# A fused two-layer Flamingo block on one core: late side products copied out in their own step, expert matrices loaded as halves

## What is computed

```
x = x + tanh(g0) * xattn0(ctx, x)            # 8 heads, masked
x = x + tanh(g2) * moe(x)                    # w1, w3 [8,512,256], w2 [8,256,512]
      h1 = x w1^T ; h3 = x w3^T ; y = (silu(h1) * h3) w2^T, weighted by the router
x = x + tanh(g1) * xattn1(ctx, x)            # 16 heads
x = x + tanh(g3) * ffn(x)                    # act_quant / weight_quant, conv, gelu
```

## Time and profile before

| | us |
|---|---|
| median of 3 runs | 1510.13 (1507.44 to 1515.85) |
| the profiled execution | 1512.02 |
| its span, first to last instruction | 1510.3 |

### The profile page before, as it was taken

How to read it: one execution, slowest core, us unless ns; L and a number is a source line. 1 busy time by engine, 2 the same in 40 slices (tenths; PEclk the granted TensorE clock), 3 DMA queues, 4 the chain that set the end, 5 groups by cost and what they waited for, 6 DMA issues and landing times.

```text
span 1510.3 us, 45214 instructions
## 1 busy us (share of the span) xinstructions
PE 1266.9 (84%) x16920; PEld 984.6 (65%) x16920; DVE 1059.2 (70%) x2851; ACT 981.6 (65%) x2319; POOL 1087.2 (72%) x1346
## 2 busy tenths in 40 slices
PE   1888888678987878788999999899999999998863
PEld 1556665567766756556888787667666667666652
DVE  4777878856555567786666666777877778777645
ACT  2887877555555566545656565787777777777741
POOL 5887876767666654465777677788888888878763
PEclk9998989889999989989999999999999999999985
DMA  8689888589999958358999997454544544355320
GB/s 254 145 233 209 181 205 183 138 169 240 225 245 229 226 111 200 97 118 214 248 269 240 251 250 189 82 108 96 100 89 95 102 96 107 85 93 100 78 53 7
DMA packets 444426, 239.97 MB, mean 159 GB/s; under 512 B 389312, under 2 KB 423984, under 8 KB 436400
## 3 DMA queue, kind: packets, MB, share of 16 engines
q1 hardware_dynamic: 411720, 178.51, 57.5%
q10 hardware_dynamic: 29416, 51.22, 10.7%
q0 software_dynamic: 3072, 7.34, 1.8%
HBM read 107.78 MB, written 35.50 MB: 95 GB/s over the span
## 4 chain that ended last, share of the span: by engine, by line
PE 34%; ACT 17%; DVE 12%; issue 10%; DMA 9%; POOL 7%; SPq 5%; DVEq 3%; ACTq 2%; POOLq 0%; another core or an unknown queue 0%
PE bank_ring L1144 7%; DMA expert_up<-experts_up 6%; PE bank_ring L1182 5%; PE bank_ring L1130 5%; DVE scores L1411 5%; ACT scores L900 5%; PE bank_out L1163 4%; PE bank_x L1245 4%; ACT probs L907 3%; ACT values L927 3%; PE bank_scores L1104 2%; SPq L555 2%; POOL probs L692 2%; PE bank_x L1196 2%; ACT keys L920 2%
## 5 line engine op out<-in xcount | busy, mean ns | idle before, releaser
L692 POOL TENSOR_TENSOR probs<-scores,probs 112x487 f16<-112x487 f32 x373 | 414.1, 1127 | 221.7 <-ACT probs L907 217.0
L900 ACT ACTIVATE scores<-scores,score_min 112x487 f32<-112x487 f32 x384 | 266.3, 695 | 117.4 <-DVE score_min L1411 114.5
L1433 DVE SCALAR_TENSOR_TENSOR values<-bank_ring,values 128x512 f16<-128x512 f32 x192 | 132.4, 690 | 214.4 <-ACT values L927 214.0
L1411 DVE CUSTOM_DVE_ANT_0 scores<-bank_scores,mask 112x487 f32<-112x487 f32 x384 | 238.3, 658 | 2.5 <-PE bank_scores L1104 2.1
L907 ACT ACTIVATE probs<-scores 112x487 f16<-112x487 f32 x384 | 214.2, 606 | 17.1 <-DMA probs_turned<-probs 1.1
L927 ACT ACTIVATE values<-bank_ring 128x512 f16<-128x512 f32 x192 | 113.2, 590 | 134.6 <-PE bank_out L1163 132.5
L1144 PE MATMUL bank_ring<-weights,kv_B 128*128 128x128 f16 x3072 | 194.8, 220 | 2.1 <-DVE keys L1428 2.1
L1144 PEld LDWEIGHTS bank_ring<-weights,kv_B 128*128 128x128 f16 x3072 | 183.9, 99 | 11.3 <-DVE keys L1428 3.2
L1163 PE MATMUL bank_out<-values,probs_turned 128*128 128x64 f16 x4608 | 170.8, 195 | 17.1 <-issue 16.8
L1130 PE MATMUL bank_ring<-kv_B,weights 128*128 128x488 f16 x768 | 180.9, 372 | 0.0
L1163 PEld LDWEIGHTS bank_out<-values,probs_turned 128*128 128x128 f16 x4608 | 159.0, 99 | 20.7 <-issue 19.1
(11 more groups left out here) (236 smaller groups left out, 2424.9 us busy)
## 6 DMA issues: line engine op xcount, KB each, us to landing
expert_up<-experts_up SPq DMA_DIRECT2D x43, 1024.0 KB
expert_down<-experts_down SPq DMA_DIRECT2D x43, 512.0 KB, 6.7
raw_weights<-in_weights ACTq DMA_DIRECT2D x8, 1536.0 KB, 10.8
experts_up<-expert_up ACTq DMA_DIRECT2D x8, 1024.0 KB, 5.3
probs_turned<-probs SPq DMA_TRANSPOSE x384
context_turned_B<-kv_B ACTq DMA_DIRECT2D x16, 375.0 KB, 7.8
kv_B<-context_turned_B ACTq DMA_DIRECT2D x16, 375.0 KB, 4.0
moe_results<-moe_result SPq DMA_DIRECT2D x43, 128.0 KB, 4.4
```

Of the source, the lines that this page charges most:

```text
L692: pool.tensor_tensor(PR[:, u % 4, 1, 0:KEYS], S[:, u % 4, 0:KEYS], PR[:, u % 4, 0, 0:KEYS], ALU.subtract).then_inc(probs_split[u % 2], 1)
L900: act_e.activation(S[:, u % 4, 0:KEYS], S[:, u % 4, 0:KEYS], ACT.Exp, bias=rmin[:, u % 4:u % 4 + 1], scale=-1.0, accum_out=rsum[:, g % 2, ...
L1411: dve.tensor_tensor_reduce(out=S[:, u % 4, 0:KEYS], in0=bS[u % 2][0:TOK, 0:KEYS], in1=mask[:, m, 0:KEYS], scale=1.0, scalar=3.0e38, op0=AL ...
```

## The change

Two things, and what they need.

1. DVE reads the late products of step j in step j itself, behind the keys' split and ahead of `split_v(j)`, and no longer behind the masks of step j+1. The five small instructions behind the second `f_max` become a function `hidden_scale`; it stays in step j+1 (now behind `norm_out`), but for the last two sequences, where it stays with the read.
2. The up matrices of an expert are kept so that a first half (columns for the first 256 hidden units of w1 and w3) and a second half are each contiguous per partition, and are loaded with two DMAs of 512 KB and a semaphore each. The second half of tile i+1 is issued where the whole was. The first half of tile i+2 is issued in step i, between the two transposes of the probabilities. PE waits for each half on its own. The rounding and splitting of expert weights write two runs of 256 columns.

```diff
-                if part == 0:
+                if part < 2:
                     if t >= 2:
-                        sp.wait_ge(up_ready, 2 * (t - 2) + 2)
-                    sp.dma_start(eup[:, t % 2], up_dram[e]).then_inc(up_loaded[t % 2], 16)
+                        sp.wait_ge(up_ready, 2 * (t - 2) + part + 1)
+                    at = part * UP_WORDS // 2
+                    sp.dma_start(eup[:, t % 2, at:at + UP_WORDS // 2], up_dram[e][:, at:at + UP_WORDS // 2])\
+                        .then_inc(up_loaded[t % 2][part], 16)
...
                     if i == -2:
                         load_expert(b, 0, 0)
+                        load_expert(b, 0, 1)
                     if i == -1:
-                        load_expert(b, 0, 1)
+                        load_expert(b, 0, 2)
...
                     if 1 <= i + 1 < TILES[b]:
-                        load_expert(b, i + 1, 0)
+                        load_expert(b, i + 1, 1)
                     if 1 <= i < TILES[b]:
-                        load_expert(b, i, 1)
+                        load_expert(b, i, 2)
...
                 if is_pair(j):
-                    for u in (2 * j, 2 * j + 1):
-                        turn_probs(u)
+                    turn_probs(2 * j)
+                    for b in range(2):
+                        i = j - first_tile_step(b)
+                        if 1 <= i + 2 < TILES[b]:
+                            load_expert(b, i + 2, 0)
+                    turn_probs(2 * j + 1)
...
+                pe.wait_ge(up_loaded[t % 2][half], 16 * (t // 2 + 1))
                 if half == 0:
-                    pe.wait_ge(up_loaded[t % 2], 16 * (t // 2 + 1))
                     pe.wait_ge(xt_loaded[t % 2], 16 * (t // 2 + 1))
...
-                            at = (2 * (2 * mat + kb) + a) * CHUNK + 128 * m
+                            at = (8 * half + 2 * (2 * mat + kb) + a) * (CHUNK // 2) + 128 * (m % 2)
...
+            def hidden_scale(n):
+                dve.drain()
+                dve.tensor_scalar(fs[:, 5:6], fs[:, 3:4], fs[:, 4:5], 2 * QMIN_SCALE, ALU.max, ALU.max)
+                dve.drain()
+                dve.reciprocal(fs[:, 6:7], fs[:, 5:6])
+                dve.tensor_scalar(fs[:, 5:6], fs[:, 5:6], qfac[0:TOK, 1:2], None, ALU.mult)
+                dve.drain()
+                dve.tensor_scalar(fs[:, 6:7], fs[:, 6:7], QMAX, None, ALU.mult).then_inc(rate_ready, 1)
...
-                    if j == 1:
...
+                    if j == 1 and n >= NSEQ - 2:
+                        hidden_scale(n)
...
                 if is_pair(j + 1) and not halves_in_step(j - 1):
                     split_k(j + 1)
-                for t in late(j - 1):
-                    part(t)
                 for g in range(PAIRS // 4):
                     if slack(g) and j == 4 * g + 6:
                         norm_out(g)
+                for t in late(j - 1):
+                    if t[0] == "f_max" and t[2] == 1 and t[1] < NSEQ - 2:
+                        hidden_scale(t[1])
                 if is_pair(j + 2):
                     split_q(j + 2)
...
                     split_probs(2 * j + 1)
+                for t in late(j):
+                    part(t)
                 if halves_in_step(j):
                     split_v(j)
```

More of the change, by code:

```diff
@@ L441, in build @@
         scattered = [sem("scattered_0"), sem("scattered_1")]
-        up_loaded = [sem("up_loaded_0"), sem("up_loaded_1")]
+        up_loaded = [[sem(f"up_loaded_{i}{half}") for half in range(2)] for i in range(2)]
         down_loaded = [sem("down_loaded_0"), sem("down_loaded_1")]
@@ L463, in expert_half @@
             if i < 4:
-                return eup[:, e % 2, (2 * i + part) * CHUNK:(2 * i + part + 1) * CHUNK]
-            return edown[:, e % 2, (2 * i - 8 + part) * CHUNK:(2 * i - 7 + part) * CHUNK]
+                return eup[:, e % 2].rearrange("p (h q c) -> p h q c", h=2, c=CHUNK // 2)[:, :, 2 * i + part]
+            at = (2 * i - 8 + part) * CHUNK
+            return edown[:, e % 2, at:at + CHUNK].rearrange("p (h c) -> p h c", h=2)
         def expert_raw(c):
             e, i = c // MOE_CHUNKS, c % MOE_CHUNKS
-            return raw[:, e % 2, i * CHUNK:(i + 1) * CHUNK]
+            return raw[:, e % 2, i * CHUNK:(i + 1) * CHUNK].rearrange("p (h c) -> p h c", h=2)
         def raw4(i):
@@ L1713, in part @@
                                       apply_absolute_value=True).then_inc(x1_drained, 1)
-                    if j == 1:
-                        dve.drain()
-                        dve.tensor_scalar(fs[:, 5:6], fs[:, 3:4], fs[:, 4:5], 2 * QMIN_SCALE, ALU.max, ALU.max)
-                        dve.drain()
-                        dve.reciprocal(fs[:, 6:7], fs[:, 5:6])
-                        dve.tensor_scalar(fs[:, 5:6], fs[:, 5:6], qfac[0:TOK, 1:2], None, ALU.mult)
-                        dve.drain()
-                        dve.tensor_scalar(fs[:, 6:7], fs[:, 6:7], QMAX, None, ALU.mult).then_inc(rate_ready, 1)
+                    if j == 1 and n >= NSEQ - 2:
+                        hidden_scale(n)
                 elif name == "f_rate":
```

## The result

The changed kernel takes **1463.2 us** (median of 4 runs, 1462.0 to 1466.0) against 1508.8 on the same chip: ratio 0.970, interval 0.966 to 0.974. The forecast was 1458 with a range of 1433 to 1494; faster had 0.88. A second set of runs of the same kernel, on another chip and beside other runs of before, gave 1467.2 and 0.975 (0.972 to 0.978).

The account below looks back on a forecast made before the run. No engine was full over the whole span; in plain layer 1 the chain of ACT and DVE would bind. 21 + 7.7 + 4.4 + 5.7 + 3.9 + 7.1 + 2.9 = 52.7 us off 1512.0, less 1.9: 1458 us, range 1433 to 1494.

Parts of the forecast that it names:

- Plain layer 1: Ten sequences, steps 104 to 184: 46.9 to 44.8 us each, 21 us in all, out of three listed PE waits totalling 32.0.
- the round of ACT and DVE: Plain layer 1: mask, exponentials, keys, probabilities, values, split, next mask; eight rounds 39.7 us plus 5.1 other ACT work, 44.8.
- The added wait: DVE stands at step end for PE's late product; costed at nothing, covered by 0.98 us idle a step before `split_v`.
- the gain of 9.6 us in layer 0: Layer 0 ahead of its tiles: half of the router's 11.3 us wait, 5.7, and a quarter of the context transpose's 15.6, 3.9.
- The router's term: Tiles of layer 0: PE's queries no longer wait for the router's product, taken in full, 7.7 us.
- The load's term: Tiles of layer 0: 60% of PE's 11.8 us of waits for the up matrices goes, 7.1 us.
- The tiles of layer 1: Steps 80 to 104: 60% of PE's 4.9 us of waits for the up matrices goes, 2.9 us.
- Between the tiles: Steps 56 to 80: about half of the router's 8.8 us of waits reaches the chain, 4.4 us.
- The slower one: Tile steps: the third load makes SP's queue the bound, 1.8 us on 43 steps; 1554 us, chance 0.07.
- the queue takes what the halves give: Tiles: the queue takes the halves' gain and the router's part there; 35.0 us stay, 1477 us, chance 0.14.
- PE all the way: Whole kernel: ACT's extra work fits its gaps, the queue keeps up, every listed wait goes, 92.1 us; 1420 us, chance 0.08.
- the chain takes all: Outside tiles the added wait eats the cover; only the tiles' 17.7 us stay, 1494 us, chance 0.13.

Follow-up runs that it names:

- values_first: Changed kernel, but ACT rounds the values before the convolution and before the latents of layer 1: 1455.9 us, ratio 0.969.
- halves_alone: Kernel before with only the up matrices' halves, the first issued a step sooner; late products still read behind the next masks: 1499.7 us, ratio 0.995.
- late_alone: Kernel before with only the late products read in their own step; up matrices loaded whole: 1478.6 us, ratio 0.982.
- one_number: Changed kernel, but the expert's number is read once per tile and kept in a register for its three loads: 1462.8 us, ratio 0.969.
- halves_together: Changed kernel, but both halves of tile i+1 are issued where the whole was, without the early start: 1488.0 us, ratio 0.986.
- store_later: Changed kernel, but ACT issues an expert's store and the next raw load two steps later in layer 0: 1458.4 us, ratio 0.973.

## Why the prediction was right, and where it was not

**Plain layer 1: right in size and cause.** 44.8 us a sequence was forecast, 44.67 came; 21 us, and 20.4 came. The waits did not go as listed. Two of the three went, the third is still there by half (4.9 of 9.6), and a fourth of 5.4 us went that I had left out. PE's waits of the stretch fell from 39.5 to 23.2 us, and the rest was kept back by the round of ACT and DVE, as costed. Three runs bear the cause: more ACT work is paid to four fifths, more PE work to little over one fifth, and taking ACT tasks out of the round without removing them gives 0.85 us. That the round's 5.1 us of extras is exactly the right sum is not shown; the sum was met within 0.13. Both estimates lie close: `values_first` reaches 43.82, next to the 43.7 that PE was to need, but PE still waits there (POOL's mask 9.0 us in nine, the heads 4.5 in ten), so PE's own floor is lower than the one I worked out. It was worked out from three waits of four: with the fourth it is 43.7 - 0.5 = 43.2.

**The added wait: right where it was costed, missed where it was not.** In layer 1 the cover was 0.98 us a step, and about half of it was used. I priced the cover from layer 1's rows alone and took the same zero for layer 0. There DVE's wait for PE's late product reached 3.13 us, because PE itself stood for the transposed probabilities, 12.2 us in all, and ACT stood 20.8 us for them. That is **the step that failed: the gain of 9.6 us in layer 0 (5.7 for the router, 3.9 for the context)**. I saw the waits of the earlier trace rows and asked who waits behind them, not what PE's late products stand behind in PE's own order. Measured: -2.6 us in the profiled execution, of which some 6 belong to part 2 in step 38 (`halves_alone` against before), so part 1 by itself lost there: `late_alone` takes 246.2 against before's 244.5, and over the kernels with halves the loss is some 8 us.

**The tiles of layer 0: near, by two misses that cancel.** 14.8 was forecast, 11.9 came (12.4 with step 38). The router's term was too large: its waits are gone, but taking them away is worth 1.8 us alone and 2.2 beside part 2, not 7.7, since PE then stands longer in later steps (43 and 47 in `late_alone`). The load's term was too small: part 2 is worth 9.7 alone, not 7.1. So the sum of these terms was met by luck. Each of these lengths is from one execution; six kernels with both parts and the same order here lie between 173.7 and 178.9.

**The tiles of layer 1:** 2.9 forecast for the loads and nothing for part 1; 4.5 came. `late_alone` has 4.1 of it (225.6 in steps 80 to 104) and `halves_alone` 1.2. The load's waits are gone in full, not to 60%, and yet part 2 by itself is worth less than half of what I gave it; the gain is mostly part 1's, which I had at nothing.

**Between the tiles:** 4.4 forecast; PE came 9.3 us earlier up to step 79, and 4.0 were given back in step 79, which grew from 11.5 to 15.5 us: PE waits 5.6 us ahead of the first up product, and the transpose of the first rows is issued 5.5 us into the step where it was 3.4. It is as long in `halves_alone`, where PE had not come earlier, so an early PE is not the whole cause; why the rows are issued late is open. Some 2.2 of the 4.0 are the clock: behind the longer wait (5.6 us, before 2.5) it is 0.56, and the up product, the heads and the values take 2.72, 0.95 and 2.19 us where they took 1.50, 0.55 and 1.50.

**The tail and the start:** 5.4 us that I did not cost. 3.5 of it is in the last eight steps, which run the same round (49.6 to 46.0 in seven of them).

**A slip of the sum.** 1512.0 - 52.7 - 1.9 is 1457.4, so the forecast should read 1457; nothing hangs on it.

**The rivals.** The slower one, SP's queue as the bound at 1554 us, did not come: the third load costs 1.3 us of the queue, and the transposes behind it became shorter by 0.5 a pair, but both sets of tiles got shorter, by 16.4 us together, and one read of the expert's number instead of three changes nothing (`one_number`). With that the rival *the queue takes what the halves give* falls too. The rule of the Trainium skill ("DMA: Bandwidth & Descriptors", section "Bandwidth") to batch to at least 1 MiB would have cost an estimated 86 us by that page's fixed time, which it gives for DMAs that GpSimd issues ("Anatomy of one DMA"), while these are issued by SP. The trace does not show such a cost in the time of a step: with loads of 512 KB the tile steps got shorter. `halves_together` shows what is true in the rival: without the early start the 24 tile steps with the same three loads are 15.9 us longer. *PE all the way* fell with the round, *the chain takes all* with the 42.3 us of idle time still left ahead of the values' split.

## What to carry to other kernels

When a read is moved to the end of its own step, the engine that reads takes on every wait that the writer has ahead of that product. Price this in each stretch by what the writer stands behind there, not once by the best-covered stretch. Two waits of one engine in neighbouring steps are seldom a sum: take one away alone, in thought, and see whether the other grows. List every wait of the stretch before you work out an engine's own pace. And where ACT and DVE are the round that bounds, try to move work out of the round before you remove any: here 4.0 us of ACT's work moved gave 0.85.

## What the runs showed of the hardware that I had not expected

Transposing DMAs on SP's queue were held back by large DMAs that another engine had queued: two took 8.05 us to issue, one of them 5.79 by itself, and the next three 6.24 while ACT's queue was moving a store and a raw load, where 1.25 us is the time of one in layer 1. With these large DMAs issued two steps later, the transposes of the old place took 1.23 to 1.26 us (`store_later`). From issue to landing the chain of waits gives the second of the held pair 13.26 us. In the tiles, with 1 MB ahead of the first of them instead of 1.5, one transpose took a mean of 1.64 us instead of 1.88. So the time of a small transpose depends on what large transfers were issued shortly before it, from its own queue or another, and a pair took up to three times as long.
